# Feed-forward on one core: magic numbers of x to ScalarE, epsilon to GpSimd, VectorE's statistics and x's grid at other places of the turn

## The reference

```python
def fp4_quant_dequant(x):                     # BLOCK = 16
    xb = x.reshape(shape[:-1] + (shape[-1] // BLOCK, BLOCK))
    scale = jnp.max(jnp.abs(xb), axis=-1, keepdims=True) / 6.0
    scale = jnp.maximum(scale, jnp.float32(1e-12))
    idx = jnp.searchsorted(_MID, jnp.abs(xb / scale))
    q = _GRID[idx] * jnp.sign(xb / scale) * scale

gate, y = fp4_linear(x, w_gate), fp4_linear(x, w_up)
h = jax.nn.silu(gate) * y
return fp4_linear(h, w_down)
...
x = x + 0.5 * _L0_ffn_ref(_layernorm(x), Wg, Wu, Wd)
x = x + _L0_attn_ref(_layernorm(x), Wq, Wk, Wv, Wo, bo)   # 16 heads of 8, causal
x = x + 0.5 * _L0_ffn_ref(_layernorm(x), Wg, Wu, Wd)
```

## Time and profile before

| what | value |
|---|---|
| median of 3 runs | 553.6 us (553.4 to 554.84) |
| profiled execution | 553.63 us |
| its span in the trace | 551.6 us |
| TensorE busy | 449.4 us (81%) |
| VectorE busy | 433.7 us (79%) |
| ScalarE busy | 311.7 us (57%) |
| GpSimd busy | 250.9 us (45%) |

### The profile page before, as it was taken

One profiled execution on the slowest core, in us unless ns is written; L12 is line 12 of the kernel. 1 busy time (PEld: TensorE's weight loads), 2 busy tenths in 40 slices (PEclk: granted clock), 3 DMA queues, 4 the chain that ended last, 5 costly groups with the idle time before them and its releaser, 6 DMA issues.

```text
span 551.6 us, 12999 instructions
## 1 busy us (share of the span) xinstructions
PE 449.4 (81%) x3689; PEld 318.3 (58%) x3689; DVE 433.7 (79%) x1212; ACT 311.7 (57%) x745; POOL 250.9 (45%) x448
## 2 busy tenths in 40 slices
PE   0557788778467899999999999999888677777885
PEld 0335565556364566766766676677555455555564
DVE  6599999998516678777777788778656999999882
ACT  1335555544333377777777777777576455545542
POOL 5334444344332265555555655554453444444421
PEclk9989898999777599999999999999999899989898
DMA  7000000000144544444444443441000000000000
GB/s 214 13 1 3 0 0 0 0 0 0 34 121 133 141 119 127 121 129 108 110 127 125 124 124 106 111 117 51 3 4 2 1 21 19 19 10 19 19 20 29
DMA packets 28460, 33.40 MB, mean 61 GB/s; under 512 B 1667, under 2 KB 25219, under 8 KB 26115
## 3 DMA queue, kind: packets, MB, share of 16 engines
q1 hardware_dynamic: 28419, 32.89, 21.9%
HBM read 21.91 MB, written 10.49 MB: 59 GB/s over the span
## 4 chain that ended last, share of the span: by engine, by line
PE 38%; issue 27%; DVE 20%; POOL 8%; ACT 5%; DMA 1%; POOLq 1%; DVEq 1%; ACTq 0%
PE bank L946 6%; PE bank L943 5%; PE bank L988 5%; POOL hq_out L409 5%; DVE nm L775 5%; PE bank L974 4%; PE bank L923 3%; PE bank L885 2%; PE bank L992 2%; PE bank L855 2%; DVE hq_normed L633 2%; PE bank L930 1%; DVE hq_amax L622 1%; PE bank L856 1%; PE bank L1018 1%
## 5 line engine op out<-in xcount | busy, mean ns | idle before, releaser
L775 DVE TENSOR_REDUCE nm<-bank 128x2 f32<-128x512 f32 (+1 forms) x192 | 128.8, 686 | 38.1 <-PE bank L946 35.2
L444 POOL TENSOR_SCALAR_AFFINE_SELECT probs<-probs 128x256 f32<-128x256 f32 (+1 forms) x192 | 91.4, 486 | 67.1 <-ACT probs L567 63.2
L567 ACT ACTIVATE probs<-bank 128x512 f32<-128x512 f32 x192 | 108.6, 596 | 21.9 <-PE bank L974 20.7
L885 PE MATMUL bank<-wdT,f_hT 128*128 128x128 f32 (+1 forms) x384 | 61.7, 300 | 35.7 <-ACT f_hT L512 35.6
L946 PE MATMUL bank<-k_stack,q_stack 72*128 72x256 bf16 (+1 forms) x512 | 78.3, 256 | 0.0
L885 PEld LDWEIGHTS bank<-wdT,f_hT 128*128 128x128 f32 (+1 forms) x384 | 51.0, 202 | 45.7 <-ACT f_hT L512 28.5
L855 PE MATMUL bank<-wguT,f_xT 128*128 128x352 f32 x128 | 58.4, 542 | 20.9 <-ACT f_xT L494 20.9
L974 PE MATMUL bank<-q_stack,k_stack 75*128 75x256 bf16 (+1 forms) x512 | 67.6, 249 | 4.1 <-ACT probs L567 3.3
L943 PE MATMUL bank<-causal,ident_bf 128*128 128x256 bf16 (+1 forms) x192 | 63.1, 328 | 4.0 <-DVE nm L775 3.6
L475 ACT ACTIVATE hq_magic<-hq_exps 128x704 bf16<-128x704 bf16 x32 | 25.3, 790 | 66.1 <-DVE hq_exps L642 66.1
L398 POOL TENSOR_TENSOR fln_mean_neg<-fln_mv,minus_one 128x2 f32<-128x2 f32 x32 | 6.5, 205 | 122.1 <-DVE fln_var_eps L672 121.1
(11 more groups left out here) (113 smaller groups left out, 925.8 us busy)
## 6 DMA issues: line engine op xcount, KB each, us to landing
q_stack<-q_parts SPq DMA_DIRECT2D x16, 576.0 KB
k_stack<-k_parts SPq DMA_DIRECT2D x16, 576.0 KB
q_parts<-qk_parts SPq DMA_DIRECT2D x16, 192.0 KB, 2.1
k_parts<-qk_parts SPq DMA_DIRECT2D x16, 192.0 KB, 2.4
k_parts<-qk_parts SPq DMA_DIRECT2D x16, 128.0 KB, 2.3
out_dram<-x_all SPq DMA_DIRECT2D x16, 128.0 KB, 1.8
q_stack<-nmT SPq DMA_DIRECT2D x16, 24.0 KB
x_all<-in_L_attn_X_dram SPq DMA_DIRECT2D x1, 256.0 KB, 2.9
```

The costliest lines, as they stand in the source:

```text
L444: nc.gpsimd.affine_select(out=v, in_=v, compare_op=ALU.is_ge, fill=0.0, base=0, pattern=[[0, heads], [1, P]], channel_multiplier=-1).then_ ...
L567: nc.scalar.activation(probs[:, c, :], ps[:, :], ACT.Exp, scale=SCALE).then_inc(done, 1)
L775: nc.vector.tensor_reduce(nm[:, j, h0:h0 + n], ps[:, :].rearrange("p (h k) -> p h k", h=n), AX_X, ALU.max, negate=True).then_inc(done, 1)
L885: last = nc.tensor.matmul(ps.dn[:, C * j:C * j + C], f_hT[0:k, t, P * j:P * j + P], wdT[0:k, t, :], start=(t == 0), stop=False)
```

## The change

Four edits, all in how the feed-forward's norm and quantisers are spread over engines and over the turn:

- The epsilon is added by GpSimd (a third small instruction in inverse_std, with a wait of its own), in attention too. norm_variance goes, LNSTEPS is 4 instead of 5.
- x's magic number is made by ScalarE, in a new step xo ahead of h's (now called hm).
- hq on VectorE is split: hq takes the maxima, scales and reciprocals, hn the normalised values, odd and exps, x's now ahead of h's. lnS stands behind that.
- x's sum becomes a step xs behind lnS. x's grid becomes a step xg at the end of the turn, behind h1. xr and hr keep their places on GpSimd.

The diff, cut to its core:

```diff
 FFN_LAG = {step: lag for lag, steps in enumerate((
     "lnS lnA lnE lnN",
-    "xq xr",
+    "xq xo xs xg xr",
     "xT gu0 h0 gu1 h1",
-    "hq hr",
+    "hq hn hm hr",
     "hT0 hT1 dn",
 )) for step in steps.split()}
-FFN_ORDER = "xT lnS hq lnA lnE xq gu0 xr hr h0 hT0 gu1 lnN hT1 dn h1".split()
+FFN_ORDER = "xT hq hn xo hm lnS xs lnA lnE xq gu0 xr hr h0 hT0 gu1 lnN hT1 dn h1 xg".split()
+FFN_AHEAD = FFN_LAG["hq"] - FFN_LAG["xq"]
...
-    LNSTEPS = 2 * NT + 1
+    LNSTEPS = 2 * NT
...
                 nc.gpsimd.tensor_tensor(ln.mean_neg[:, :], ln.mv[:, :, 0], minus_one[:, :], ALU.mult).then_inc(ln.mean_neg_ready, 1)
+                nc.gpsimd.tensor_tensor(ln.var_eps[:, :], ln.mv[:, :, 1], eps[:, :], ALU.add).then_inc(ln.var_ready, 1)
                 if not first(n, 1):
                     pool.wait_ge(ln.out_ready, NT * n)
+                pool.wait_ge(ln.var_ready, n + 1)
                 nc.gpsimd.tensor_tensor(ln.rstd[:, :], ln.var_eps[:, :], half_power[:, :], ALU.pow).then_inc(ln.rstd_ready, 1)
...
+                def magic_x(b, s, it):
+                    if not first(b, FFN_AHEAD):
+                        magic(xquant, b + base)
...
-                steps = {"xT": x_copy, "lnN": x_norm, "xq": magic_weights,
-                         "hq": lambda b, s, it: magic(hquant, b + base), "dn": down}
+                steps = {"xT": x_copy, "lnN": x_norm, "xq": magic_alone, "xo": magic_x,
+                         "hm": lambda b, s, it: magic(hquant, b + base), "dn": down}
...
-                for q, s, n in jobs:
-                    if q is xquant:
-                        dve.wait_ge(q.step, QSTEPS * n + QEXPS)
-                        nc.vector.tensor_scalar(q.magic[:, :], q.exps[:, :], MAGIC_MUL, MAGIC_ADD, ALU.mult, ALU.add).then_inc(q.magic_ready, 1)
...
+            def add_magic(q, n):
+                dve.wait_ge(q.magic_ready, n + 1)
+                nc.vector.tensor_tensor(q.sum[:, :], q.odd[:, :], q.magic[:, :], ALU.add).then_inc(q.step, 1)
+
+            def take_grid(q, s, n):
+                wait_step(q, n, QSUM)
+                nc.vector.tensor_tensor(q.grid[:, s, :], q.sum[:, :], q.magic[:, :], ALU.subtract).then_inc(q.step, 1)
...
             def norm_stats(ln, n, b):
+                if not first(n, 1):
+                    dve.wait_ge(ln.step, LNSTEPS * n)
                 for j in range(NT):
                     nc.vector.bn_stats(ln.stats[:, j, :], x_all[:, b, j, :]).then_inc(ln.step, 1)
...
-            def norm_variance(ln, n):
-                dve.wait_ge(ln.step, LNSTEPS * n + 2 * NT)
-                nc.vector.tensor_scalar(ln.var_eps[:, :], ln.mv[:, :, 1], EPS, None, ALU.add).then_inc(ln.step, 1)
...
+                def scale_both(b, s, it):
+                    h = h_job(b, s)
+                    take_amax(*h)
+                    if alone(b):
+                        take_scale(*h)
+                        take_inverse(*h)
+                    else:
+                        x = x_job(b + FFN_AHEAD, (s + FFN_AHEAD) % FFN_UNROLL)
+                        take_amax(*x)
+                        take_scale(*h)
+                        take_scale(*x)
+                        take_inverse(*h)
+                        take_inverse(*x)
+
+                def bits_of_both(b, s, it):
+                    n, x = b + base, b + base + FFN_AHEAD
+                    if not alone(b):
+                        normalise_blocks(xquant, s, x, fln.out[:, (s + FFN_AHEAD) % FFN_UNROLL, :], None)
+                    normalise_blocks(hquant, s, n, f_h[:, :, :].rearrange("p j i -> p (j i)"), None)
...
+                def sum_x(b, s, it):
+                    if not first(b, FFN_AHEAD):
+                        add_magic(xquant, b + base)
+
+                def grid_x(b, s, it):
+                    if not first(b, FFN_AHEAD):
+                        take_grid(xquant, s, b + base)
...
-                         "xq": quantise_x, "xr": round_x, "hq": quantise_both, "hr": round_both}
+                         "xq": quantise_x, "xr": round_x, "hq": scale_both, "hn": bits_of_both, "xs": sum_x, "xg": grid_x,
+                         "hr": lambda b, s, it: round_fp4((hquant, s, b + base))}
```

More of the change, by code:

```diff
@@ L236, in __init__, with blocks_of @@
                 self.ready = sem(f"{n}_ready")
+            def blocks_of(self, values):
+                return values.rearrange("p (n k) -> p n k", k=BLOCK)
         class NormBuffers:
@@ L242, in __init__ @@
                 self.mean_neg = sb(f"{n}_mean_neg", [P, NT])
+                self.var_ready = sem(f"{n}_var_ready")
                 self.out = sb(f"{n}_out", [P, turns, NT * C])
@@ L383, in _ @@
             nc.gpsimd.memset(minus_one[:, :], -1.0).then_inc(consts, 1)
+            nc.gpsimd.memset(eps[:, :], EPS).then_inc(eps_ready, 1)
             nc.gpsimd.memset(ident[:, :], 0.0).then_inc(consts, 1)
@@ L387, in _ @@
             pool.wait_ge(consts, 5)
+            pool.wait_ge(eps_ready, 1)
             nc.gpsimd.affine_select(out=ident[:, :], in_=ident[:, :], compare_op=ALU.not_equal, fill=1.0,
@@ L477, in ffn, with magic_alone @@
             def ffn(base, ps):
-                def magic_weights(b, s, it):
+                def magic_alone(b, s, it):
                     if not base and first(b, 1):
                         magic(wquant, 0)
+                    if first(b, FFN_AHEAD):
+                        magic(xquant, b + base)
+                def magic_x(b, s, it):
+                    if not first(b, FFN_AHEAD):
+                        magic(xquant, b + base)
                 def x_norm(b, s, it):
@@ new lines, in wait_step, with take_amax, take_scale @@
+            def wait_step(q, n, k):
+                dve.wait_ge(q.step, QSTEPS * n + k)
+            def take_amax(q, s, n, src, released):
+                nc.vector.tensor_reduce(q.amax[:, :], q.blocks_of(src), AX_X, ALU.max, apply_absolute_value=True).then_inc(q.step, 1)
+            def take_scale(q, s, n, src, released):
+                wait_step(q, n, 1)
+                if released:
+                    dve.wait_ge(*released)
+                nc.vector.tensor_scalar(q.scale[:, s, :], q.amax[:, :], 1.0 / 6.0, SCALE_MIN, ALU.mult, ALU.max).then_inc(q.step, 1)
@@ new lines, in take_inverse, with normalise_blocks @@
+            def take_inverse(q, s, n, src, released):
+                wait_step(q, n, QSCALE)
+                nc.vector.reciprocal(q.inv[:, :], q.scale[:, s, :]).then_inc(q.step, 1)
+            def normalise_blocks(q, s, n, src, released):
+                wait_step(q, n, QINV)
+                nc.vector.scalar_tensor_tensor(out=q.blocks_of(q.normed[:, :]), in0=q.blocks_of(src), scalar=BELOW_ONE,
+                                               in1=q.inv[:, :].unsqueeze(2).to_broadcast([P, q.blocks, BLOCK]),
+                                               op0=ALU.mult, op1=ALU.mult).then_inc(q.step, 1)
@@ new lines, in take_odd, with take_exps @@
+            def take_odd(q, n):
+                wait_step(q, n, QNORMED)
+                upper = q.normed[:, :].bitcast(I16).rearrange("p (n two) -> p n two", two=2)[:, :, 1]
+                nc.vector.tensor_scalar(q.odd[:, :].bitcast(I16), upper, 1, None, ALU.bitwise_or).then_inc(q.step, 1)
+            def take_exps(q, n):
+                wait_step(q, n, QODD)
+                nc.vector.tensor_scalar(q.exps[:, :].bitcast(I16), q.odd[:, :].bitcast(I16), EXP_BITS, None,
+                                        ALU.bitwise_and).then_inc(q.step, 1)
@@ new lines, in add_magic @@
+            def add_magic(q, n):
[4 more added lines that the diff above has]
+                nc.vector.tensor_tensor(q.grid[:, s, :], q.sum[:, :], q.magic[:, :], ALU.subtract).then_inc(q.step, 1)
+            def quantise(*jobs):
+                for step in (take_amax, take_scale, take_inverse, normalise_blocks):
+                    for job in jobs:
+                        step(*job)
+                for step in (take_odd, take_exps):
+                    for q, s, n, src, released in jobs:
+                        step(q, n)
@@ L645, in round_fp4 @@
             def round_fp4(*jobs):
                 for q, s, n in jobs:
-                    if q is xquant:
-                        dve.wait_ge(q.step, QSTEPS * n + QEXPS)
-                        nc.vector.tensor_scalar(q.magic[:, :], q.exps[:, :], MAGIC_MUL, MAGIC_ADD, ALU.mult, ALU.add).then_inc(q.magic_ready, 1)
+                    add_magic(q, n)
                 for q, s, n in jobs:
-                    dve.wait_ge(q.magic_ready, n + 1)
-                    nc.vector.tensor_tensor(q.sum[:, :], q.odd[:, :], q.magic[:, :], ALU.add).then_inc(q.step, 1)
@@ L654, in round_fp4 @@
-                for q, s, n in jobs:
-                    dve.wait_ge(q.step, QSTEPS * n + QEXPS + 1)
-                    nc.vector.tensor_tensor(q.grid[:, s, :], q.sum[:, :], q.magic[:, :], ALU.subtract).then_inc(q.step, 1)
+                    take_grid(q, s, n)
             def norm_stats(ln, n, b):
+                if not first(n, 1):
```

(4 more changed lines are left out.)

54 lines of the change are left out of this document (12 added, 42 removed).

## The result

The changed kernel takes 583.17 us (median of 6 runs, 582.23 to 588.45) against 554.04 us of the kernel before (6 runs, 553.27 to 554.84). The medians are 29.1 us apart, 5.3%. The ratio on record is 1.0605, 95% interval 1.0551 to 1.0659: slower. The forecast was 575.8 with a range of 557 to 588.

The account below looks back on a forecast made before the run. VectorE's chain was taken as the bound in the feed-forwards; 24 turns x 0.78 + 3 half-clock turns x 0.5 = +20.2, plus 2 for the clock, on 553.6 gives 575.8 us, range 557 to 588.

Parts of the forecast that it names:

- The block on h's scale: VectorE's scale of h falls inside GpSimd's rescale of h and waits for its end: 0.86 us a turn, bounds 0 and 0.86.
- VectorE's own sum: VectorE's steps in a full feed-forward turn without the block: 7.40 - 0.37 + 0.11 + 0.10 + 0.08 = 7.32 us.
- the gain of 0.08 in VectorE's own work: A full feed-forward turn of VectorE falls from 7.40 to 7.32 us, before the block is added.
- The clock: Term for TensorE being granted half speed more often, as its busy share falls to 0.72: +2 us taken.
- The half-clock turns: Feed-forward turns with TensorE at half speed: 9 instead of 3, 8.36 us becoming 8.7 to 9.0.
- the second ring: Feed-forward chain of statistics, GpSimd, ScalarE's norm, down-projection, next x, gate and up, SiLU; close behind VectorE's chain, loses 0.3 to 0.6.
- the same there: The two statistics (0.40 us) move from behind f_h to behind the exponents, cost VectorE the same there and cover ScalarE.
- The norm's ring: The second ring, through the feed-forward's norm: loses 0.3 to 0.6 us against a turn growing 0.78, not binding in ordinary turns.
- faster: Rival: the rescale doesn't keep h's scale out at the head of the turn; 551.4 us, or 549; chance 0.10.
- Slipping in: Rival: h's scale starts before GpSimd's rescale and x's normalise waits 0.2 instead; 556.8 us (551 to 562.5); chance 0.07.
- The clock in almost every turn: Rival: TensorE's clock falls in almost every feed-forward turn, 27 x 0.5 = 13 us on 573.8, about 587; chance 0.08.
- ScalarE too slow: Rival: x's magic on ScalarE costs as much as h's, +0.37 us a turn, 10 us more, 586; chance 0.05.

Follow-up runs that it names:

- e1: The changed kernel with x's grid moved back ahead of h's sum; 569.83 us, ratio 1.0287 to the kernel before.
- e2: The kernel before with x's grid alone moved to the turn's end; 571.41 us, ratio 1.0328.
- e5: The changed kernel with eight extra 128x256 bf16 matmuls a turn on TensorE as filler; 581.51 us, ratio 1.0475 to the kernel before.
- e3: The changed kernel with GpSimd doing h's rescale ahead of x's rescale; 577.07 us, ratio 1.0402 to the kernel before.
- e4: The changed kernel with h's rescale cut into two GpSimd instructions of 352 columns; 571.21 us, ratio 1.0310 to the kernel before.
- e6: The kernel before with eight extra 128x256 bf16 matmuls a turn on TensorE as filler; 554.72 us, ratio 1.0009.
- e11: The kernel before with the epsilon add alone moved to GpSimd, in feed-forwards and attention; 550.33 us, ratio 0.9971.
- e9: The changed kernel with x's grid early and the two statistics back behind f_h; 556.66 us, ratio 1.0034 to the kernel before.

## Why the prediction was right, and where it was short

- **The block on h's scale** (the largest term, 0.86 a turn, taken at its upper end): right. The scale took 1.04 instead of 0.18, 0.86 to 0.87 more, and ended with the rescale in the changed kernel, e1, e2 and e5. hq_out started 1.81 behind the first f_h (464.57 against 462.76), as worked out. The lower bound, no wait for a two-input multiply, is out. The Trainium skill (SBUF — State Buffer, "Who interferes with whom") states an exclusive lock for the whole instruction; the runs agree, with 0.86 for the scale, with 1.15 for x's grid in e3, and with e4, where the wait shrank with the instruction.
- **VectorE's own sum**, 7.32 and 8.18 with the block: nearly right. At full clock (e5) the two turns of the unrolled loop take 8.14 and 8.22 in feed-forward 2, a mean of 8.18, but 8.14 and 8.34 in feed-forward 1. Over the 22 turns the growth was 0.86 a turn where the sum had 0.78, so the gain of 0.08 in VectorE's own work didn't come. Two holes on VectorE stand in its place: 0.08 ahead of the aggregates in each turn of the loops, and 0.23 instead of 0.11 ahead of the first f_h in every second turn of feed-forward 1; what causes the second stays open. x's magic on ScalarE took 0.42, the estimate from two rows; h's sum came 0.21 behind the start of the aggregates in this turn, and no wait for ScalarE is left in most turns.
- **The miss of 7 us** has three parts. The sum had 22.2 us, the span grew by 29.4. Ordinary turns: 18.9 over the 22 (e5 against e6), where the sum had 22 x 0.78 = 17.2, so 1.7. The clock: 2.9, where the sum had 2 less 0.28 for each of three turns, 1.2, so 1.7. Outside the 22 turns: 7.6, where the sum had five turns of 0.78, 3.9, so 3.7, half of the miss.
- **The half-clock turns**: I had worked out nine in place of three, and ten came in the 22 turns and two more outside them. Each takes 0.55 to 0.8 more than the same turn with the filler, near the 8.7 to 9.0 us that the second ring gave. But +2 was taken where nine gave +3, and 2.9 was the net. The way to the nine was luck: it tied the clock to TensorE's busy share, with the ramp as nearest row. e3 has longer turns and TensorE less busy in its second stretch (65.08 of 93.21 us), and its clock is 0.96 there; in its first (68.77 of 92.64) it is 0.91.
- **Outside the 22 turns**: the turns of the feed-forwards there grew by 1.8 us together. 1.6 stand ahead of the first rescale of h, 3.3 between the last rescale of feed-forward 1 and the first of feed-forward 2, 0.9 behind the last rescale. The forecast took 0 for attention. e11 shows no cost of epsilon there, but the scatter of that stretch over the profiles is larger than the 3.3, so its cause stays open.
- **The count of what the statistics cost by their move**: the working said "the same there". For VectorE's own work that is right. But they were the cover of h's rescale, and e1 against e9 prices them, with the norm that comes later behind them, at 14 us. In the sum it was inside the 0.86, since with both x's grid and the statistics moved the block is paid once; as an account of causes it was missing, and so e1's forecast of 549 to 552 was 18 us off.
- **The norm's ring**: said not to bind in ordinary turns, and it doesn't; in the 22 turns VectorE waits for SiLU in half-clock turns only, for 0.45 to 0.69. That the norm on GpSimd, itself held up by VectorE's sum and grid, delays the rescale behind it in the queue was not in the working. The epsilon add was near 0.15 + 0.08 in my estimate and 0.48 where h's sum ran beside it.
- **The rivals**: faster, out. Slipping in, out in the changed kernel: the rescale was ahead by 0.39. The clock in almost every turn: it fell in every second one, and that is 1.7 of the 7 us. ScalarE too slow: out. The measured 583.17 is at the upper edge of the forecast's own range, 567 to 583.
